# The bias of z in a Mamba-2 and routed-attention kernel: its product's operands with 128 rows in place of 33

## The reference, cut to what matters

```python
def _mamba2_block(x, ln_w, ln_b, in_proj_w, conv_w, conv_b, A_log, D, dt_bias, gamma, out_proj_w):
    u = _layernorm(x, ln_w, ln_b)
    zxbcdt = u @ in_proj_w.T
    z = zxbcdt[..., :D_INNER]
    ...
    y = y * jax.nn.silu(z)
    y = y * jax.lax.rsqrt(jnp.mean(y * y, -1, keepdims=True) + EPS) * gamma
    return x + y @ out_proj_w.T
```

## Time and profile before

| | us |
|---|---|
| median of 3 executions | 3877.43 |
| lowest and highest | 3871.91, 3879.42 |
| the profiled execution | 3869.49 |
| its span | 3867.8 |
| mean granted TensorE clock in it | 0.971 of full speed |

### The profile page before, as it was taken

The page is one execution under the profiler, slowest core; times in us unless marked ns, Lnnn a source line. Parts: engine busy times, 40 slices in busy tenths (PEclk is TensorE's granted clock), DMA queues, the critical chain, the costliest instruction groups (busy, mean ns, idle before and its releaser), DMA issues.

```text
span 3867.8 us, 72420 instructions
## 1 busy us (share of the span) xinstructions
PE 3607.0 (93%) x28354; PEld 2160.3 (56%) x28354; DVE 2962.5 (77%) x5342; ACT 2539.6 (66%) x4781; POOL 1838.9 (48%) x1483
## 2 busy tenths in 40 slices
PE   4899999999999999999857999999999999999998
PEld 2455555555555555555434666555565566656655
DVE  3788897878889887888967766777777776777664
ACT  4677777777777777775445666676666756666665
POOL 0233333323333332322337778776655755665565
PEclk7899999999999999999978999999999999999999
DMA  4233333324233233322354334444333433333333
GB/s 122 71 79 65 74 77 70 83 74 88 64 72 72 75 85 75 88 64 42 66 72 122 64 73 73 79 99 86 71 82 66 104 81 68 70 78 76 71 61 43
DMA packets 297669, 294.27 MB, mean 76 GB/s; under 512 B 38664, under 2 KB 222600, under 8 KB 295281
## 3 DMA queue, kind: packets, MB, share of 16 engines
q1 hardware_dynamic: 241008, 186.70, 19.6%
q0 software_dynamic: 56320, 102.94, 15.1%
HBM read 176.19 MB, written 101.71 MB: 72 GB/s over the span
## 4 chain that ended last, share of the span: by engine, by line
PE 79%; DVE 9%; POOL 4%; issue 3%; DMA 3%; ACT 2%; SPq 0%; DVEq 0%; POOLq 0%; ACTq 0%
PE pair L1234 10%; PE pair L1280 8%; PE pair L1317 8%; PE pair L1365 7%; PE pair L1480 6%; PE pair L1327 6%; PE pair L1394 4%; PE pair L1380 4%; PE pair L1308 3%; PE pair L1299 2%; PE pair L1440 2%; PE pair L1441 2%; DVE smx L1880 2%; PE pair L1410 2%; PE pair L1289 1%
## 5 line engine op out<-in xcount | busy, mean ns | idle before, releaser
L1626 DVE SCALAR_TENSOR_TENSOR cv<-raw,taps,cv 128x512 f32<-128x512 f32 x480 | 429.4, 905 | 66.6 <-ACT cv L2039 63.4
L2323 POOL TENSOR_TENSOR ph<-pf,ph 128x512 f16<-128x512 f32 x256 | 366.3, 1431 | 197.8 <-ACT ph L2183 196.0
L1880 DVE TENSOR_REDUCE smx<-pair 128x2 f32<-128x514 f32 x512 | 349.0, 684 | 101.4 <-PE pair L1410 101.1
L1234 PE MATMUL pair<-xhT,whi 128*128 128x512 f16 x1280 | 384.0, 382 | 0.2
L1913 DVE TENSOR_TENSOR ph<-pf,ph 128x512 f16<-128x512 f32 x256 | 265.2, 1036 | 101.0 <-ACT ph L2183 100.9
L1280 PE MATMUL pair<-zhi,xhT 128*128 128x512 f16 x1024 | 325.7, 379 | 1.2 <-ACT ob L2101 1.2
L1317 PE MATMUL pair<-ohi,yT 128*128 128x512 f16 x1024 | 318.5, 383 | 1.1 <-ACT yT L2096 1.1
L2069 ACT ACTIVATE de<-de,cum 128x128 f32<-128x128 f32 x1024 | 309.9, 390 | 1.0
L2177 ACT ACTIVATE pf<-pair 128x1024 f32<-128x1024 f32 x256 | 262.0, 1023 | 42.4 <-PE pair L1441 36.2
L2317 POOL DMA_INDIRECT y<-res,slot_i x128 | 206.0, 1609 | 140.0 <-ACT res L2202 124.2
L2183 ACT CAST ph<-pf 128x1024 f16<-128x1024 f32 x256 | 268.5, 1049 | 4.9
(11 more groups left out here) (272 smaller groups left out, 10517.9 us busy)
## 6 DMA issues: line engine op xcount, KB each, us to landing
de<-cum SPq DMA_DIRECT2D x64, 1024.0 KB, 9.5
rows<-rowt SPq DMA_DIRECT2D x16, 1040.0 KB, 5.5
xin<-x SPq DMA_DIRECT2D x16, 1024.0 KB, 7.4
y<-xin SPq DMA_DIRECT2D x16, 1024.0 KB, 4.6
y<-ob POOLq DMA_DIRECT2D x64, 256.0 KB, 4.3
qb<-qa SPq DMA_DIRECT2D x32, 512.0 KB
rbc<-rank SPq DMA_DIRECT2D x63, 256.0 KB, 3.4
wst<-wkv SPq DMA_DIRECT2D x32, 256.0 KB, 3.2
```

The costliest lines, as they stand in the source:

```text
L1234: ins = pe.matmul(bk[:], w[:, k, ws], xt[:, ha, k, :], start=n == 0, stop=n == 3 * KD - 1)
L1626: ve.scalar_tensor_tensor(c_[:], r_[:, t:t + BLK], taps[:, ct, t:t + 1], c_[:], ALU.mult, ALU.add).then_inc(done, 1)
L1880: ve.tensor_reduce(smx[:, qt, 2 * h2:2 * h2 + 2], sc[:, :, 0:NK + 1], AX.X, ALU.max)
L2323: po.tensor_tensor(p_[:, 1, 1], f[:, 1], p_[:, 0, 1], ALU.subtract).then_inc(S.plp, 1)
```

## The change

Two tiles of the setup are declared with P = 128 rows. The memsets and the product take whole tiles (`[:]`), so they cover 128 rows from now on; the added rows of `z_bias` hold zeros, those of `ones` ones. The values of z stay the same.

```diff
@@ -981,8 +981,8 @@
             slo = sb(mam, "slo", [P, KD, NSM], F16)
             ohi = sb(mam, "ohi", [P, KI, D], F16)
             olo = sb(mam, "olo", [P, KI, D], F16)
-            z_bias = sb(mam, "z_bias", [33, DI], F16)
-            ones = sb(mam, "ones", [33, P], F16)
+            z_bias = sb(mam, "z_bias", [P, DI], F16)
+            ones = sb(mam, "ones", [P, P], F16)
             dt_b = sb(mam, "dt_b", [P, NH], F32)
             a_neg = sb(mam, "a_neg", [P, NH], F32)
             d_bc = sb(mam, "d_bc", [P, NH], F32)
```

## The result

The changed kernel takes 3834.9 us (five executions, 3833.6 to 3839.1), the kernel before beside it 3874.7 us (five, 3871.9 to 3879.4): ratio 0.9898, 95% interval 0.9883 to 0.9912, so 1.0% faster. Two later series of the same kernel gave 0.9904 (0.9887 to 0.9921) and 0.9894 (0.9878 to 0.9911).

A forecast was written before the change was run, and what follows sets the result against it. TensorE was taken to bound the Mamba stage: (13.3 + 16.9) x 118/128 = 27.8 us saved, with setup, absorption and clock at 0, so 3877.4 - 27.8 = 3849.6 us; 8-in-10 range 3840 to 3862 us.

The forecast's parts named there:

- The bound and the mechanism: Mamba stage: TensorE bounds it; weights of 33-row bias products and their successors aren't loaded ahead, 54.2 us idle in all.
- The product itself and the group behind it: At L1282 and its following group: 13.3 us saved on the 128 products, 16.9 us on the groups behind.
- On the path: Mamba stage: 118 of the 128 bias products count towards the kernel's time, so 27.8 us are saved.
- The setup: Two memsets now covering 128 partitions: taken as 0 us extra, with +1.9 us as upper bound.
- What is late next: Gate waiting for yhl: cover shrinks 0.4 to 0.6 us per chunk, 0.8 us spare; none of the gain absorbed.
- The clock: TensorE's granted clock, 300 to 1800 us: taken as 0 since the pauses stay, bounds -15 and +15 us.
- The base: Whole kernel: the starting time was 3877.4 us, the median of three timed runs.
- the stretch from the first to the last L1282: Sign in the changed profile, Mamba stage: this stretch gets shorter by some 28 to 30 us.
- Rows don't matter: At L1282: its place causes the gaps, which would stay at 128 rows; 3877 us, chance 0.06.
- Absorbed: Mamba stage: the y chain or VectorE takes up the thinner cover, half given back; 3863 us, chance 0.08.
- Slower, by the clock: TensorE pauses longer and works at 1.2 GHz more often; 3892 us with 25 further stretches, chance 0.03.
- More than forecast: TensorE's pauses get short enough that the clock stays up; 3835 us, chance 0.06.

The follow-up runs named there:

- fill128: The changed kernel with one more full 128-row product per half of z, its result overwritten; ratio to the kernel before 0.9985.
- twice33: The kernel before with the bias product moved first in each half of z and another 33-row product ahead of it; 3881.1 us, ratio 1.0042.
- first33: The kernel before (33 rows) with the bias product first instead of last in each half of z; 3857.8 us, ratio 0.9986.
- rows64: The kernel before with the two tiles at 64 rows in place of 33; ratio to the kernel before 0.9997.
- rows65: The kernel before with the two tiles at 65 rows in place of 33; ratio to the kernel before 0.9906.
- nobias: The changed kernel with the bias product of z left out; ratio to the kernel before 0.9825.
- short33_2: The kernel before (33 rows) with two zlo products left out of each half of z; 3809.6 us in a single execution, 0.9854 of the kernel before.
- short33_1: The kernel before (33 rows) with one zlo product left out of each half of z; ratio to the kernel before 0.9895.
- hold7: The changed kernel with nine full products filling each of TensorE's seven pauses ahead of the gate, results overwritten; ratio to the kernel before 0.9884.

## Why the prediction was wrong in size

**The bound and the mechanism: right.** TensorE bounds the stage in the kernel before, the waits grew by 2 us only, and what L1282 cost was in the starts. (The seven waits stand in every second block, 226 us apart, not in each one as the prediction says; their sum is unaffected.) That 33 and 64 rows pay while 72 and 128 don't was read from four shapes and held to one row.

**The product itself and the group behind it:** 13.3 + 16.9 = 30.2 us predicted, 30.5 measured: 12.3 ahead of the bias product, 13.1 between it and its successor, 5.2 inside the group behind. The prediction's pieces go by ends and mine here by starts, so only the sums compare. L1244, which I had called the weakest part with 1.3 us, gave 1.4: 0.7 at its start and 0.7 inside.

**On the path:** I counted 118 of 128. The chain of the kernel before has 124: the first two stand on it, and four of the eight behind 1842 us. So 30.5 x 124/128 = 29.5 us, and 1.4 us were left out without need. That is by the chain; the times can't confirm it. The table has the kernel before at 260.5 us from the last logits to the attention and the changed one at 252.2 to 256.0, where its 14 products are worth 3.3 us, but fill128 with 14 products more than the changed kernel takes 256.3 and twice33 with 14 more than first33 takes less. That stretch moves by some 4 us for reasons that stay open; its time at half clock moves too (61.4 us before, 58.0 and twice 64.9 after).

**The setup:** 0, right: 485 ns as before. **What is late next:** right for the gates, 14.3 us in seven waits in both. Missed was L1299, which waits for `yT` (L2096): 2 us, and the chain's 60 us over VectorE and ScalarE in every second block.

**The clock: the step that failed.** "I take 0, since the pauses stay." The pauses stayed, seven of 2.04 us; the falls behind them did not, from seven to four or six, and none of 6.8 us where two had been. Time at half clock went from 32.9 us to 13.7 (12.8 and 19.6 in the later profiles), worth 5.6 to 8.4 us. I had bounded it by 15 us and given the whole of it 0.06. That the pauses stay was no reason for the falls to stay: rows64, with the old timing, repeats all of them, and the changed kernel doesn't even repeat its own. A part of the bound belonged into the range on both sides. Alone this term would have given 3849.6 - 8.1 = 3841.5 us, still inside the range; with the base, the path and what is left over the time fell out of it.

**The base:** the three runs' median was 3877.4 us, that of five 3874.7.

The sum with these: 3874.7 - 29.5 - 8.1 + 2.0 = 3839.1 us, and 3834.9 was measured. The 4.2 us left are not explained; the ratio's interval is wider (0.9883 to 0.9912 is 11 us), and from one series to the next it moves by 4 us (0.9894 to 0.9904). Of the signs named ahead, the stretch from the first to the last L1282 was to be 28 to 30 us shorter and is 41.3 us shorter (34.8 and 31.6 in the later profiles).

**The rivals.** "Rows don't matter" fell with rows65. "Absorbed" is true of 2 us of waits here and not of half the gain; nobias shows that the next step would lose more. "Slower, by the clock" didn't come: no kernel of the table spends more at half clock than the one before, though short33_2 has 7.7 us more than short33_1 and twice33 6.4 more than first33. "More than forecast" named 3835 us, and 3834.9 was measured, but that is luck: its condition, pauses short enough for the clock to stay up, wasn't met (they kept their 2.04 us), and the clock's part was some 8 us, not 15.

## What to carry to other kernels

In a stream of full products, look at the distance between starts and at whether a weight load stands ahead of its product or with it: durations showed 2% here (387 against 379 ns), where the starts showed 0.2 to 0.3 us lost per product. A product with a short contraction among full ones is cheaper padded with zeros to more than 64 rows (shown here for f16 with 512 columns), if the stream is what bounds the kernel, and if several are needed they belong side by side. After each such saving look at the chain again: here one step brought the other engines to a near tie. A pause of a few us in a dense stream has a second price in the clock behind it; it differs from kernel to kernel and from one execution to the next, so give it a range rather than a value.

## What the runs showed of the hardware

A switch between products of 33 or 64 rows and full ones, f16 with 512 columns, costs 0.096 us on the way in and 0.102 us on the way out at 2.4 GHz (before against after), and a further 0.10 us if the group behind is f32 (L1308 1.82 us between starts against 1.72). The step lies between 64 and 65 rows (rows64, rows65). Two products of the small kind follow each other at 0.22 to 0.23 us (twice33). A memset of VectorE takes the same 485 ns for 33, 64, 65 and 128 rows. Seven pauses of TensorE of 2.04 us (2.18 in nobias) were followed by stretches at 1.2 GHz after every one in before, rows64 and fill128, after four or six in the changed kernel, after none in nobias, and filling them removed all (hold7); each us at half clock cost 0.42 us in this mixed stream, an estimate from hold7 against the changed kernel. What tells the pauses apart stays open.
